# The first expert-choice call's norm, scores and choice of tokens for four sequences, worked out among units 47 to 68 of the mixture ahead of it

## The chip, the cores and the metric

The kernel is one program on one core of a Trainium2 chip. Its engines run side by side, each in the order of its own instruction list: TensorE (PE, matmuls and transposes into PSUM), VectorE (DVE), ScalarE (ACT), GpSimd (POOL) and SyncE (SP, which issues DMAs). They wait for one another only at semaphores. The metric is device time in microseconds (us), lower is better. Kernels are compared by the median of several runs. Where it ran, a profiled execution gives the time of each instruction.

## The reference

2048 tokens (8 sequences of 256) of width 128 go through six layers: a mixture of experts, a linear attention, the same mixture again, an expert-choice layer, a causal attention, and the expert-choice layer again. Every layer has a layer norm ahead of it and is added to the stream `x`. The second mixture and the first expert-choice call are the place of this change:

```python
x = x + 0.5 * _L0_ffn_ref(_layernorm(x, axis=-1), ...)   # 8 routed experts, 2 per token, and a shared one
x = x + 0.5 * _L1_ffn_ref(_layernorm(x, axis=-1), ...)   # expert choice
...
def _L1_ffn_ref(x, gate_w, w1, w2):
    scores = jnp.einsum('ntd,ed->nte', x, gate_w)
    probs = jax.nn.softmax(scores, axis=-1)
    g, m = jax.lax.top_k(probs.transpose(0, 2, 1), k)     # each expert takes 64 of a sequence's 256 tokens
    xin = x[batch_idx, m]
    h = jnp.einsum('nekd,edf->nekf', xin, w1)
    ...
```

A sequence's choice depends on that sequence's tokens alone, so four of the eight sequences can be chosen as soon as the mixture has finished those four.

## The kernel before

The stream lies as `xr`, 128 features by 2048 tokens, in four blocks of 512 tokens (two sequences each). An instruction such as "128x512" covers one block.

**The mixture** is `ffn0`, called twice. Its work is a list of 72 units: 8 of the shared expert, then 16 for each block in order (8 experts, two halves of the hidden width). A unit goes round all engines. PE does `up` (six matmuls, `L128` to `L130`), ScalarE a silu (`gate`, `L1290`), VectorE multiplies it with the second product (`product`, `L1755`) and by the token's weight (`weigh`, `L1762`), ScalarE rounds it to the matmul's short form (`high`, a cast, `L1299`), GpSimd subtracts to get the rest (`L2174`), and PE does `down` (three matmuls) four units later. `up(n)` waits until `product(n - 2)` has emptied its PSUM banks. When a block's last unit is down, VectorE adds the block to `xr` (`add`, `L1766`): block 0 behind the product and weighing of unit 29, block 1 of unit 45, block 2 of unit 61, block 3 after the end.

**The first expert-choice call** is `ffn1`, and its head already stands at the end of the second `ffn0`. For a block it needs: centred tokens (`ln_centre`, a matmul), their square and a copy (ScalarE, `ln_square`, `ln_copy`), the variance and the gate's scores (`ln_variance` and `scores` on PE, many narrow matmuls), and the tokens turned round and scaled (`rows_turned` on PE, then ScalarE, then a subtraction on GpSimd). For four sequences (a part, blocks 0 and 1 or 2 and 3) it then needs: the inverse root (`ln_root`, eleven small operations of VectorE) and the scores less their maximum (`part_weights`), the exponential (ScalarE, which has to load another table of functions), the division (`chances`), a transpose on PE, and the choice on VectorE: `top_start`, eight `top_rounds` of three operations each (the eight largest, their places, and their removal), `top_end`. PE turns the result back (`tops`) and spreads it (`indices`), VectorE copies it into columns (`columns`) and makes the one-hot matrices (`select`), and with these PE picks the tokens (`gather`), from which the experts' matmuls start.

Before, the head for blocks 0 and 1 starts at units 68 and 69 of the mixture (centre on PE, square and copy on ScalarE); variance and scores stand between the last four downs; everything from the root on comes after the last unit, and 28 `spare` matmuls, whose results nobody reads, stand ahead of `tops`.

The order on each engine is the order in which its function issues the instructions, so the position of a call in a loop is the only thing that sets it. The numbers after "L" in rows of before are lines of the kernel printed here.

## Time and profile before

| | |
|---|---|
| median of 3 runs | 1073.49 us (1071.27 to 1079.22) |
| profiled execution, its own time | 1074.08 us |
| its span on the core | 1072.4 us |
| PE busy | 959.2 us (89%) |
| VectorE busy | 706.4 us (66%) |
| ScalarE busy | 619.3 us (58%) |
| GpSimd busy | 338.7 us (32%) |

A busy share is a mean over stages with different limits. The second mixture lies between about 493 and 651 us, the join to the expert-choice call between about 640 and 684 us. A row of the timeline gives the start, the length, the engine, the line, the operation, its output and inputs and their sizes; what ended the engine's idle time stands in brackets. Matmul rows overlap, because matmuls are pipelined: their starts tell the pace. fp32 matmuls count twice in the trace where they take two passes, so 8 narrow ones are "x16". A row that covers several instructions runs from the start of the first to the end of the last.

### The profile page before, as it was taken

What the parts mean: (1) busy time and instruction counts of PE and PEld (TensorE: products, weight loads), DVE (VectorE), ACT (ScalarE), POOL (GpSimd) and SP (SyncE); (2) the same over time, 40 slices, a digit from 0 to 9 for tenths busy, and PEclk for the clock granted to TensorE, in tenths of its full rate; (3) what the DMA queues carried; (4) which work ended last, traced back from release to release, by engine and by line L of the source; (5) the groups of instructions that cost most, each with busy time, mean ns of one, the idle gap of its engine ahead of it and who ended that gap; (6) DMA issues with size and microseconds to landing.
All of it is one profiled execution on the core that took longest, in us unless ns stands there. A gap on an engine that the chain in (4) does not pass through costs nothing.

```text
span 1072.4 us, 13356 instructions
## 1 busy us (share of the span) xinstructions
PE 959.2 (89%) x4674; PEld 636.4 (59%) x4674; DVE 706.4 (66%) x1413; ACT 619.3 (58%) x1003; POOL 338.7 (32%) x249
## 2 busy tenths in 40 slices
PE   8899999889999999889999998899977878787997
PEld 5678887333333333357888875688544545454886
DVE  3978887577877787546888877634375455438532
ACT  6555555378888888653555553635644545445454
POOL 1697777100000000003777764201201211123200
PEclk9999999999999999888999998899988888889999
DMA  5225120000000000004321211100000000001001
GB/s 173 50 76 162 60 66 23 0 0 1 1 1 1 0 1 1 0 1 135 76 67 59 63 37 60 40 2 1 1 2 2 4 2 2 4 1 40 1 1 40
DMA packets 30745, 33.66 MB, mean 31 GB/s; under 512 B 2063, under 2 KB 19799, under 8 KB 30679
## 3 DMA queue, kind: packets, MB, share of 16 engines
q1 hardware_dynamic: 30678, 32.81, 10.6%
q8 instruction: 37, 0.61, 0.2%
q14 instruction: 30, 0.24, 0.1%
HBM read 31.36 MB, written 1.18 MB: 30 GB/s over the span
## 4 chain that ended last, share of the span: by engine, by line
PE 50%; DVE 20%; ACT 11%; POOL 11%; issue 8%; DMA 0%; SPq 0%; ACTq 0%; POOLq 0%; DVEq 0%
POOL fl L2174 9%; PE ps L128 6%; PE ps L129 6%; PE ps L130 6%; PE ps L760 5%; PE ps L878 4%; PE ps L754 2%; ACT ex L1504 2%; ACT L1393 2%; PE ps L738 2%; DVE smax L2053 2%; PE ps L972 2%; PE ps L907 1%; DVE stk L2045 1%; PE ps L981 1%
## 5 line engine op out<-in xcount | busy, mean ns | idle before, releaser
L2174 POOL TENSOR_TENSOR fl<-fp,fh 128x512 fp32r<-128x512 f32 x144 | 224.1, 1573 | 123.5 <-ACT fh L1299 123.4
L1290 ACT ACTIVATE fs<-ps 128x512 f32<-128x512 f32 x144 | 86.3, 599 | 112.7 <-PE ps L130 112.5
L1762 DVE TENSOR_TENSOR fp<-fp,cwb 128x512 f32<-128x512 f32 x128 | 140.3, 1096 | 14.0 <-DVE fp L1755 0.9
L1755 DVE TENSOR_TENSOR fp<-fs,ps 128x512 f32<-128x512 f32 x144 | 98.1, 682 | 39.4 <-ACT fs L1290 39.0
L128 PE MATMUL ps<-z_hi,w_hi 128*128 128x512 f32 x288 | 116.4, 404 | 3.3 <-DVE fp L1755 3.3
L129 PE MATMUL ps<-z_lo,w_hi 128*128 128x512 f32 x288 | 115.7, 402 | 0.0
L130 PE MATMUL ps<-z_hi,w_lo 128*128 128x512 f32 x288 | 115.2, 400 | 0.0
L1299 ACT CAST fh<-fp 128x512 fp32r<-128x512 f32 x144 | 88.8, 617 | 35.4 <-DVE fp L1762 31.0
L2238 POOL TENSOR_TENSOR ln_sq<-ln_rs 128x512 f32<-128x512 f32 x20 | 21.4, 1069 | 264.8 <-ACT ln_rs L1356 264.8
L2231 POOL TENSOR_SCALAR_AFFINE_SELECT ex<-ex 128x1024 f32<-128x1024 f32 (+1 forms) x24 | 33.4, 1403 | 158.5 <-ACT ex L1504 158.5
L2053 DVE TENSOR_REDUCE smax<-ps 128x8 f32<-128x2048 f32 (+1 forms) x24 | 54.9, 2290 | 42.0 <-PE ps L986 33.9
L878 PE MATMUL ps<-hid,w 128*128 128x256 f32 x256 | 67.3, 387 | 0.0
L128 PEld LDWEIGHTS ps<-z_hi,w_hi 128*128 128x128 f32 x288 | 55.2, 192 | 18.8 <-DVE fp L1755 5.5
L754 PE MATMUL ps<-z,wb 128*128 128x512 f32 x128 | 62.8, 618 | 2.7 <-DVE qq L1859 2.7
L1440 ACT ACTIVATE hid<-ps 128x512 f32<-128x512 f32 x64 | 38.0, 597 | 46.5 <-PE ps L130 45.7
L130 PEld LDWEIGHTS ps<-z_hi,w_lo 128*128 128x128 f32 x288 | 55.4, 192 | 12.9
L129 PEld LDWEIGHTS ps<-z_lo,w_hi 128*128 128x128 f32 x288 | 55.1, 191 | 12.5 <-issue 0.2
L128 PE MATMUL ps<-fh,w_hi 128*128 128x512 f32 x144 | 57.6, 400 | 2.9 <-POOL fl L2174 2.9
L760 PE MATMUL ps<-hid,wb 128*128 128x512 f32 x128 | 60.1, 593 | 0.0
L129 PE MATMUL ps<-fl,w_hi 128*128 128x512 f32 x144 | 56.9, 395 | 0.0
L130 PE MATMUL ps<-fh,w_lo 128*128 128x512 f32 x144 | 56.8, 394 | 0.0
L742 PE MATMUL ps<-ln_sq,mean_w 128*128 128x512 f32 x72 | 39.4, 629 | 18.7 <-ACT ln_sq L1349 18.7
(272 smaller groups left out, 2037.1 us busy)
## 6 DMA issues: line engine op xcount, KB each, us to landing
cwb<-cw_spread SPq DMA_DIRECT2D x64, 256.0 KB, 3.1
w_raw<-in_L_ffn_w_dram SPq DMA_DIRECT2D x20, 256.0 KB, 3.1
w_raw<-in_L_ffn_w_dram SPq DMA_DIRECT2D x4, 512.0 KB, 5.7
w<-in_L_ffn_w_dram SPq DMA_DIRECT2D x8, 256.0 KB, 4.8
x_tok<-in_L_attn_x_dram SPq DMA_DIRECT2D x4, 256.0 KB, 3.6
wb<-in_L_attn_W_dram SPq DMA_DIRECT2D x1, 1024.0 KB, 7.0
wb<-in_L_attn_W_dram SPq DMA_DIRECT2D x4, 256.0 KB, 3.9
out_dram<-z SPq DMA_DIRECT2D x4, 256.0 KB, 3.0
```

Of the source, the lines that this page charges most:

```text
L128: pe.matmul(out, w_hi, x_hi, start=start, stop=False)
L129: pe.matmul(out, w_hi, x_lo, start=False, stop=False)
L130: return pe.matmul(out, w_lo, x_hi, start=False, stop=stop)
L754: pe.matmul(ps[:, bank, :], wb[:, b, (4 + k) * P:(5 + k) * P], blk(z, t), start=True, stop=True).then_inc(a0_matmul[t], 1)
L760: pe.matmul(ps[:, A0_WO, :], wb[:, b, w], hid[:, k, :], start=(k == 0), stop=(k == FT - 1)).then_inc(a0_matmul[t], 1)
L878: ins = pe.matmul(ps[:, OUT1[n % 2], 0:SEQ], w2[:, e, ft * P:(ft + 1) * P], hid[:, g % RING1, f * SEQ:(f + 1) * SEQ], start=(ft == 0), sto ...
L1290: act.activation(fs[:, n % 2, :], ps[:, n % 2, :], ACT.Silu).then_inc(silu_done, 1)
L1299: act.copy(fh[:, n % RING0, :], fp[:, n % RING0, :]).then_inc(fhi_done, 1)
L1755: dve.tensor_tensor(f, fs[:, n % 2, :], ps[:, 2 + n % 2, :], ALU.mult).then_inc(prod_done, 1)
L1762: dve.tensor_tensor(f, f, cwb[:, x % CW_RING, :], ALU.mult).then_inc(weighed, 1)
L2053: dve.tensor_reduce(smax[:, s % 2, int(k > 0), :, hgs], ps[:, bank:bank + 4, :].rearrange("p g (h t) -> p g h t", h=HG if k == 0 else 2), ...
L2174: pool.tensor_tensor(fl[:, n % RING0, :], fp[:, n % RING0, :], f32(fh[:, n % RING0, :]), ALU.subtract).then_inc(flo_done, 1)
```

## The change

A constant `EARLY1 = 47` is added. The head for blocks 0 and 1 (part 0) of the first expert-choice call moves into the units from 47 on: centre on PE in unit 47, square and copy on ScalarE in 48 and 49, variance in 50, scores in 51, root and part weights on VectorE behind the weighing of 52, the exponential on ScalarE in 53 with a table load before and one behind it, chances in 54, their transposes in 55, the start of the choice in 56, its eight rounds in 57 to 64 (one behind each weighing), its end in 65, the transposes back in 67, and the columns in 68. After the last unit the transposed rows, `indices` and the head for blocks 2 and 3 are interleaved anew on PE and ScalarE, and the 28 spare matmuls are gone. The result of `tops` for part 0 lies in PSUM bank 5 instead of 3.

```diff
-        PT_AT, GI_AT = ((5, 3), (2, 3)), (3, 5)
+        PT_AT, GI_AT = ((5, 3), (2, 3)), ((5, 5), (3, 5))
...
+                elif call == 0 and n == 1:
+                    pe.wait_ge(col_done, part1(call, i) + 1)
...
-                    if call == 1 and n == ALL0 - 4:
+                    if call == 1 and n == EARLY1:
                         ln_centre(LN_FFN1, 0)
                         ln_centre(LN_FFN1, 1)
+                    if call == 1 and n == EARLY1 + 3:
+                        pe.wait_ge(lxc_copied, later(LN_FFN1, 1))
+                        ln_variance(LN_FFN1, 0)
+                        ln_variance(LN_FFN1, 1)
+                    if call == 1 and n == EARLY1 + 4:
+                        scores(LN_FFN1, 0)
+                        scores(LN_FFN1, 1)
+                    if call == 1 and n == EARLY1 + 8:
+                        chances(0, 0)
+                    if call == 1 and n == EARLY1 + 20:
+                        tops(0, 0)
...
                 if call == 1:
                     pe.wait_ge(prod_done, U + ALL0)
                     rows_turned(0, LN_FFN1, 0)
+                    indices(0, 0)
                     rows_turned(0, LN_FFN1, 1)
+                    indices(0, 1)
                     ln_centre(LN_FFN1, NTB - 1)
                     ln_variance(LN_FFN1, 2)
                     scores(LN_FFN1, 2)
-                    chances(0, 0)
                     ln_variance(LN_FFN1, NTB - 1)
                     scores(LN_FFN1, NTB - 1)
-                    spare(GI_AT[0], 28)
-                    tops(0, 0)
-                    indices(0, 0)
-                    indices(0, 1)
...
-                    if call == 1 and n == ALL0 - 3:
-                        for tb in range(SPB):
-                            ln_square(LN_FFN1, tb)
-                            ln_copy(LN_FFN1, tb)
+                    if call == 1 and n in (EARLY1 + 1, EARLY1 + 2):
+                        ln_square(LN_FFN1, n - EARLY1 - 1)
+                        ln_copy(LN_FFN1, n - EARLY1 - 1)
+                    if call == 1 and n == EARLY1 + 6:
+                        act.preload_act_table_set(LN_EXP)
+                        chances(0, 0)
+                        act.preload_act_table_set("silu_and_others")
...
                 if call == 1:
+                    rows_turned(0, LN_FFN1, 0)
                     ln_square(LN_FFN1, 2)
                     ln_copy(LN_FFN1, 2)
-                    act.preload_act_table_set(LN_EXP)
-                    chances(0, 0)
+                    rows_turned(0, LN_FFN1, 1)
                     ln_square(LN_FFN1, NTB - 1)
                     ln_copy(LN_FFN1, NTB - 1)
-                    rows_turned(0, LN_FFN1, 0)
-                    rows_turned(0, LN_FFN1, 1)
+                    act.preload_act_table_set(LN_EXP)
...
-                if call == 1:
-                    dve.wait_ge(sc_ready, part1(0, 0) + 1)
-                    ln_root(LN_FFN1, 0, SPB - 1)
-                    part_weights(0, LN_FFN1, 0)
+                    if call == 1 and n == EARLY1 + 5:
+                        dve.wait_ge(sc_ready, part1(0, 0) + 1)
+                        ln_root(LN_FFN1, 0, SPB - 1)
+                        part_weights(0, LN_FFN1, 0)
+                    if call == 1 and n == EARLY1 + 7:
+                        chances(0, 0)
+                    if call == 1 and n == EARLY1 + 9:
+                        top_start(0, 0)
+                    if call == 1 and n - EARLY1 - 10 in range(CAP // 8):
+                        top_rounds(0, 0, (n - EARLY1 - 10,))
+                    if call == 1 and n == EARLY1 + 18:
+                        top_end(0, 0)
+                    if call == 1 and n == EARLY1 + 21:
+                        columns(0, 0)
                 add(NTB - 1)
-                if call == 1:
-                    chances(0, 0)
-                    top_start(0, 0)
-                    top_rounds(0, 0, range(CAP // 8))
-                    top_end(0, 0)
...
-                columns(call, 0)
+                if call == 1:
+                    columns(call, 0)
                 select(0)
```

The first place is VectorE at the end of the mixture. Before, the last weighing is followed by root, part weights, the add of block 3 (`L1766`), chances and the choice; `gates`, `gidx` and `tk` are the choice's values, places and work table.

```order
L1762 TENSOR_TENSOR fp<-fp,cwb 128x512
...
L1644 TENSOR_TENSOR sce<-ps,ln_r 128x64
L1647 TENSOR_REDUCE scm<-sce 128x8
L1649 TENSOR_TENSOR sce<-sce,scm 128x64
L1766 SCALAR_TENSOR_TENSOR xr<-ps,xr 128x512
L1655 TENSOR_REDUCE scs<-sce 128x8
...
L1674 COPY tk<-ps 32x256
L1684 MAX gates<-tk 32x8
L1686 MAX_INDEX gidx<-gates,tk 32x8
L1688 MATCH_REPLACE tk<-gates,tk 32x256
```

Of the change, in the round units (57 and 58 are shown), one round stands behind each product and weighing:

```order
L1761 TENSOR_TENSOR fp<-fs,ps 128x512
L1768 TENSOR_TENSOR fp<-fp,cwb 128x512
L1690 MAX gates<-tk 32x8
L1692 MAX_INDEX gidx<-gates,tk 32x8
L1694 MATCH_REPLACE tk<-gates,tk 32x256
L1761 TENSOR_TENSOR fp<-fs,ps 128x512
L1768 TENSOR_TENSOR fp<-fp,cwb 128x512
L1690 MAX gates<-tk 32x8
```

The rounds, one block behind the last weighing before, are spread over eight units, and the next product of the mixture waits in VectorE's list behind each.

The second place is ScalarE. Before, the exponential of `sce` and its table load stand behind the last cast of the mixture, ahead of the turned rows (`xtf`, `xt_hi`):

```order
L1299 CAST fh<-fp 128x512 x2
L1245 ACTIVATE ln_sq<-ps 128x512
L1249 COPY z<-ps 128x512
L1334 ACT_TABLE_LOAD
L1258 ACTIVATE sce<-sce 128x64
L1245 ACTIVATE ln_sq<-ps 128x512
L1249 COPY z<-ps 128x512
L1267 ACTIVATE xtf<-ps,ln_r 128x128 x4
L1271 CAST xt_hi<-xtf 128x512
L1267 ACTIVATE xtf<-ps,ln_r 128x128 x4
```

Of the change, around unit 53 (the first silu, `fs`, is unit 53's, the one behind the loads is unit 54's):

```order
L1294 ACTIVATE fs<-ps 128x512
L1303 CAST fh<-fp 128x512
L1330 ACT_TABLE_LOAD
L1262 ACTIVATE sce<-sce 128x64
L1332 ACT_TABLE_LOAD
L1294 ACTIVATE fs<-ps 128x512
```

The exponential has moved in front of unit 54's silu, with a second load that was not there.

The third place is PE behind the mixture. Before (`L602` turns rows, `L571` centres, `L578` is the variance, `L594` the scores, `L566` a spare matmul, `L618` turns the choice back, `L634` spreads it, `L849` gathers):

```order
L602 MATMUL ps<-ident,z 128x128 x8
L571 MATMUL ps<-xr,centre 128x512
L578 MATMUL ps<-mean_w,ln_sq 128x1 x4
L594 MATMUL ps<-par,z 128x8 x4
L609 MATMUL ps<-ident,prb 32x128 x2
L578 MATMUL ps<-mean_w,ln_sq 128x1 x4
L594 MATMUL ps<-par,z 128x8 x4
L566 MATMUL ps<-ident_b 128x512 x28
L618 MATMUL ps<-ident,gates 128x32
L618 MATMUL ps<-ident,gidx_f 128x32
L634 MATMUL ps<-blockd,nsel 128x512 x2
L566 MATMUL ps<-ident_b 128x512 x5
```

Of the change:

```order
L603 MATMUL ps<-ident,z 128x128 x4
L637 MATMUL ps<-blockd,nsel 128x512
L603 MATMUL ps<-ident,z 128x128 x4
L637 MATMUL ps<-blockd,nsel 128x512
L572 MATMUL ps<-xr,centre 128x512
L579 MATMUL ps<-mean_w,ln_sq 128x1 x4
L595 MATMUL ps<-par,z 128x8 x4
L579 MATMUL ps<-mean_w,ln_sq 128x1 x4
L595 MATMUL ps<-par,z 128x8 x4
L567 MATMUL ps<-ident_b 128x512 x5
L853 MATMUL ps<-onehot,xt_hi 128x512 x2
```

What spreads the choice now stands between the turned rows; variance and scores of blocks 2 and 3 are what remains between them and the first gather.

## Rows read from the trace of the kernel before

**Rows 1.** Windows: length, busy PE, PEld, DVE, ACT, POOL, clock, DMA.
```profile
44.00:52.00 8.00, 6.30 (x27) 4.75 (x26) 7.72 (x9) 4.28 (x8) 6.71 (x4) 1.00 0.35 61
...
600.00:620.00 20.00, 20.00 (x88) 16.18 (x87) 16.54 (x21) 10.97 (x19) 15.05 (x10) 1.00 0.20 61
...
682.00:684.00 2.00, 0.00 (x0) 0.00 (x0) 1.90 (x8) 1.97 (x7) 1.57 (x2) 1.00 0.00 0
...
684.00:686.00 2.00, 1.93 (x8) 1.87 (x9) 1.93 (x8) 1.90 (x4) 2.00 (x2) 0.57 0.00 0
```

**Rows 2.** Groups by line, 516 to 634: shapes, count; busy, mean ns; idle before.
```profile
L2174 POOL TENSOR_TENSOR fl<-fp,fh 128x512 fp32r<-128x512 f32 x57 | 89.6, 1590 | 29.4 <-ACT fh L1299 29.4
...
L1762 DVE TENSOR_TENSOR fp<-fp,cwb 128x512 f32<-128x512 f32 x57 | 62.2, 1092 | 6.3 <-DVE fp L1755 0.5
...
L1299 ACT CAST fh<-fp 128x512 fp32r<-128x512 f32 x57 | 35.1, 616 | 12.0 <-DVE fp L1762 12.0
```

**Rows 3.** Timeline, VectorE, second mixture: start, length, line, operation.
```profile
593.30 0.69 DVE L1762 TENSOR_TENSOR fp<-fp,cwb 128x512 f32<-128x512 f32 x1
...
593.91 0.68 DVE L1755 TENSOR_TENSOR fp<-fs,ps 128x512 f32<-128x512 f32 x1
...
594.70 1.01 DVE L1762 TENSOR_TENSOR fp<-fp,cwb 128x512 f32<-128x512 f32 x1
...
602.87 0.67 DVE L1755 TENSOR_TENSOR fp<-fs,ps 128x512 f32<-128x512 f32 x1
...
644.64 0.68 DVE L1755 TENSOR_TENSOR fp<-fs,ps 128x512 f32<-128x512 f32 x1
```

**Rows 4.** Timeline, GpSimd and VectorE, early in the second mixture, small operations.
```profile
500.66 1.44 POOL L2174 TENSOR_TENSOR fl<-fp,fh 128x512 fp32r<-128x512 f32 x1 [0.23 <-ACT fh L1299]
...
500.66 1.59 DVE L1742 TENSOR_TENSOR oh<-iota_e,ixf 128x128 f32<-128x128 f32 x2
...
502.28 0.49 DVE L1746 TENSOR_TENSOR oh<-oh,pr 128x128 f32<-128x128 f32 x2
```

**Rows 5.** Timeline, PE, end of the second mixture and join.
```profile
635.43 1.88 PE L571 MATMUL ps<-xr,centre 128*128 128x512 f32 x4
...
644.12 1.84 PE L578 MATMUL ps<-mean_w,ln_sq 128*128 128x1 f32 x16
...
650.40 0.39 PE L130 MATMUL ps<-fh,w_lo 128*128 128x512 f32 x1
...
670.42 1.41 PE L849 MATMUL ps<-onehot,xt_hi 128*128 128x512 f32 x2
...
677.75 0.73 PE L849 MATMUL ps<-onehot,xt_hi 128*128 128x512 f32 x2 [0.84 <-DVE onehot L1928]
```

**Rows 6.** Timeline, VectorE, at the join behind the second mixture.
```profile
648.48 0.17 DVE L1612 TENSOR_SCALAR ln_v<-ps 128x8 f32<-128x8 f32 x1 [2.37 <-PE ps L594]
...
651.49 0.68 DVE L1766 SCALAR_TENSOR_TENSOR xr<-ps,xr 128x512 f32<-128x512 f32 x1
...
655.37 0.41 DVE L1674 COPY tk<-ps 32x256 f32<-32x256 f32 x1 [1.78 <-PE ps L609]
...
655.93 0.42 DVE L1684 MAX8 gates<-tk 32x8 f32<-32x256 f32 x1
...
666.73 0.68 DVE L1699 TENSOR_TENSOR blockd<-gidx_f,m 32x512 bf16<-32x512 f32 x1
...
668.30 0.17 DVE L1709 COPY icol<-ps 64x16 f32<-64x16 f32 x1
```

**Rows 7.** Timeline, GpSimd, at the join.
```profile
659.21 4.94 POOL L2191 TENSOR_TENSOR w_lo<-w_raw,w_hi 128x512 fp32r<-128x512 f32 x4
```

**Rows 8.** Timeline, ScalarE, at the join.
```profile
651.23 1.28 ACT L1334 ACT_TABLE_LOAD   x1
...
652.52 0.26 ACT L1258 ACTIVATE sce<-sce 128x64 f32<-128x64 f32 x1
...
654.34 1.16 ACT L1267 ACTIVATE xtf<-ps,ln_r 128x128 f32<-128x128 f32 x4
```

12 lines of the change are left out of this document (3 added, 9 removed).

## The prediction

> **What bounds the kernel now.** I read the groups of the second mixture first, then windows, then the timeline engine by engine over the join behind it. In the mixture's steady part PE is never idle (20.00 of 20 us) and VectorE is busy 16.54 of 20 [rows 1]: 57 units in 118 us, 2.07 us each, set by PE's nine matmuls [rows 2]. VectorE's busy share holds waiting as well as work: from weighing to product it is 0.61 us and from product to weighing 0.79, 1.40 for a unit [rows 3], but the weighing takes 1.09 us on the mean and 0.69 where nothing is in its way [rows 2, 3], so 0.40 us of each is waiting. What it waits for is GpSimd's subtraction (1.59 us each, three quarters of the unit): two small operations of VectorE that started with one of 1.44 us took 1.59, while two of the same size right behind it took 0.49 [rows 4].
>
> The join is the opposite: nothing is dense. The last down of the mixture ends at 650.40 + 0.39 = 650.79 and the first gather starts at 670.42 [rows 5], 19.6 us later. In between VectorE works alone: root and weights from 648.48 to 651.49, then the choice from 655.37 to 667.41 [rows 6]. This is what the change takes out of the join. The question is what it costs where it goes.
>
> **What is moved, and its price on VectorE.** Root and part weights 3.0 us; chances 0.8 (estimate: four small operations, 0.2 each from the 0.17 of the root's first); start of the choice 0.56; eight rounds with their two copies 10.80, `blockd` 0.68; columns, four copies of 0.17, 0.6; with the add of block 2, which was there before and is 0.68, 17.1 us stand beside the 20 units 52 to 71 [rows 6]. At 0.67 us of slack a unit (2.07 - 1.40) they could hide 13.4 at the very best; with the 0.40 of waiting, 5.4. So VectorE, not PE, sets the pace from unit 52 on. A round unit then takes about 1.40 + 1.35 = 2.75 us. The rounds themselves run beside GpSimd undisturbed: in the join they kept their pace under four subtractions of GpSimd [rows 6, 7].
>
> **PE's share.** The centring of blocks 0 and 1 (1.7 us) moves from unit 68 to 47 and is paid in both. Variance and scores, 16 small matmuls each and 1.7 us each [rows 5], leave the tail and go into units 50 and 51. By unit 52 the new kernel is 3 x 1.7 = 5.1 us behind; that is slack in which VectorE loses its backlog, for which I take 0.8 us (estimate: two mean waits of 0.40). Unit 52's product, at 602.87 before (its row names no wait for ScalarE, so VectorE was late there), so starts near 602.87 - 0.8 + 5.1 = 607.2 [rows 3].
>
> **From there to the product of unit 71.** 19 units at 1.40 are 26.6; the moved work 17.1; waiting behind GpSimd 0.40 in the 11 units without a round, 4.4 [rows 2] (in a round unit the subtraction falls under the round: weighing 0.69, cast 0.62 and a subtraction, 1.24 each where four ran alone and 1.59 here, make 2.6 to 2.9, about the unit); the root's and `blockd`'s two-input operations under a running subtraction, 1.8 (bounds 0 and 3, from the 1.1 us lost in [rows 4]). Then bubbles at units 53 to 56, 3.0: ScalarE does the exponential between two table loads, and the silu of unit 54 comes only after the second, 0.26 + 1.28 + 0.6 = 2.1 us behind the part weights, while VectorE has only product and weighing of 53 to do, 1.4: it waits 0.7. PE first waits in up(55) for the product of 53, which stands behind root and weights (4.2 us with a subtraction in the way, of which PE has two units' lead, so about 2.2), then at the transposes of unit 55 until VectorE has product, weighing and chances of 54 (2.2 and a wait of 1, less its own 0.7 of down: about 2.5). That holds back up(56), another 0.4, and probably costs a few us at the lower clock: after 682 to 684, where PE did nothing, the clock was 0.57 of full in the next 2 us [rows 1]. I put 1.9 there (bounds 0 and 9, below). Sum 52.9: the product of unit 71 starts near 660.1, before it was 644.64 [rows 3]: +15.5.
>
> The first load costs nothing, since the roots cover it; without that cover it would be 1.3 us more. In this trace a load is 1.28 us and the exponential starts 0.01 us behind it [rows 8]. The Trainium skill, page "ScalarE: Activation LUTs", section "What ACT_TABLE_LOAD costs", puts a drain of about 1.38 us behind each load, 2.66 in all. By that the second load would hold the silu 1.4 us longer, and the time would be 1079; the row shows no such gap, and I go by the row.
>
> **The waits that it adds, and who stands behind them.** PE's variance in unit 50 waits for ScalarE's copy of unit 49; ScalarE has two squares and two copies more in units 48 and 49, about 1.0 us a unit beside two instructions of 0.6, so it just keeps the pace. ScalarE's exponential waits for the part weights, and behind it stand the second load, the silu of 54 and the cast of 53, for which GpSimd and then PE wait. PE's transposes of unit 55 wait for the chances, with up(56) behind them. The transposes of the choice in unit 67 and the columns in 68 find their sources done two units earlier. SP's and GpSimd's own instructions keep their order, and the weights that they load and split at the join follow the mixture's end.
>
> **The tail.** Before, product 71 to the end of the last down took 650.79 - 644.64 = 6.15 us, with variance and scores in it. Without them the chain is product and weighing 0.79 + 0.69, cast 0.7, subtraction 1.59, three matmuls 0.9: 4.7. The mixture's end moves by 15.5 - 1.4 = +14.1.
>
> **The new join.** After the last down PE turns block 0 (0.5), and then ScalarE sets the time: turned rows of block 0 (1.16 and a cast, 1.8), square and copy of block 2 (two at about 0.5), turned rows of block 1 (1.8), square and copy of block 3 (1.0) [rows 2, 8]. PE's scores of block 3 wait for that copy and stand ahead of the gather in its order: 0.5 + 5.6 + 0.9, then five spare matmuls, about 1.8 with waits. The first gather so starts about 9.1 us after the last down instead of 19.6: -10.5. What is late next is therefore that copy, with scores, root and weights of block 3 behind it. From the first to the fourth gather it was 677.75 - 670.42 = 7.3 us [rows 5]. VectorE now waits there less for ScalarE (-1.5), but its second root falls under the four subtractions of `w_lo`, 4.94 us [rows 7], which the rounds had covered before without harm (+1.2). I take 0. The spare matmuls removed filled a wait and cost nothing.
>
> **Sum.** +14.1 - 10.5 = +3.6. The profiled execution took 1074.08 us, 0.6 above the median of 1073.49: 1077.7, so 1078.
>
> **The rivals.**
> - *The mixture swallows more (faster).* If no weighing falls under a subtraction from unit 52 on and there are no bubbles, the sum to product 71 is 26.6 + 17.1 = 43.7, the shift +6.3, at the end of the mixture +4.9, and with the 1.5 behind the gather 4.9 - 10.5 - 1.5 = -7.1: 1067. For it: slower units leave GpSimd time to finish in a round's shadow, and the weighing of 0.69 is common [rows 3]. Against it: the units between the moved pieces are as tight as before.
> - *PE's clock falls in the stretched units (slower).* With VectorE as the bound PE idles about a quarter of each round unit. If the clock goes to 1.2 GHz and stays there, a unit's nine matmuls take about 3.9 us instead of 2.1 (twice the spacing) and PE binds again at 3.9 against 2.75: 1.15 in each of eight units, +9.2, so 1087. It decides (over 1% slower) from about six such units. For it: the drop after the wait at 682 [rows 1]. Against it: from 44 to 52, in the first mixture, PE was also idle 1.70 of 8 us, and the clock stayed 1.00 [rows 1]. The Trainium skill, page "TensorE: Matmul & The Clock Gate", section "HAM oscillation — how this bites in real kernels", describes bursts of matmuls between waits that fall to the lower clock each time; this is that rule at work here, and the trace shows it only for the longer wait.
> - *The choice still ends last at the join (no change).* Then nothing is gained and the rest is as before, near 1074. VectorE works in order, so all of it is done before the weighing of unit 69; hardly possible.
>
> A bound beyond these: every one of 20 weighings waiting for two thirds of a subtraction, 1.06 us, would give 21 instead of 4.4, +17. The 57 units of [rows 2] wait 0.40 on the mean, so I leave that end outside the range.
>
> **How the numbers follow.** My forecast, the mixture paying what the join gains and a little more, 1072 to 1083: 0.55. The faster rival, 1063 to 1072: 0.22. The slower, 1083 to 1092: 0.20. No change by an idle move: 0.03. Runs of this kernel differ by up to 0.7%, so about 1% (10.7 us) is what can be told from no change. Under 1063 is reached only with a gain beyond the faster rival's own sum: 0.03. Over 1084 is most of the slower one: 0.16. Between: 0.81. The range 1068 to 1088 takes in both rivals' sums nearly and leaves out about 0.2.
>
> **What would show it.** Right: rounds standing behind weighings at units 57 to 64, unit spacing of about 2.7 there; PE waiting for products of VectorE, which it never did in this mixture's middle; two waits of over 2 us near unit 55; the last down 14 us later; the first gather 9 us behind it, behind the scores of block 3; a GpSimd subtraction beside the second root. Wrong: unit spacing still 2.1 in the rounds (the faster rival), matmul spacing doubled over several units (the slower one), or a first gather that comes 12 us or more behind the last down because scores or turned rows are later than I think.

## The result, and the profile after

The changed kernel takes 1083.64 us in the median of 20 executions (1071.75 to 1086.52), the kernel before beside it 1075.57 us (1066.23 to 1082.61). The ratio is 1.0057 with a 95% interval of 1.0031 to 1.0083: slower, by less than 1%. The forecast was 1078 in a range of 1068 to 1088. Two executions of over 2.3 ms, one of the kernel before and one of a variant, are left out of every mean, count and level below.

| | before | after |
|---|---|---|
| profiled execution, its own time | 1074.08 us | 1071.75 us |
| its span on the core | 1072.4 us | 1070.0 us |
| mean granted clock of PE over the span | 0.951 | 0.958 |

So the profiled execution of the changed kernel is the quickest of its 20, quicker than that of before, while the usual one is slower by 8 us. One profile cannot explain that. The executions of the changed kernel lie in two groups, 1072 to 1078 us and 1083 to 1087 us, and the mean granted clock goes with them: 0.949 to 0.958 in the first, 0.939 to 0.944 in the second.

Windows of the changed kernel (length, busy PE, PEld, VectorE, ScalarE, GpSimd with their instructions, clock, DMA share, GB/s), for [rows 1]:

```profile
600.00:620.00 20.00, 16.46 (x81) 13.14 (x79) 14.07 (x28) 9.87 (x17) 7.83 (x6) 0.91 0.13 40
620.00:660.00 40.00, 36.91 (x151) 27.20 (x151) 36.81 (x82) 19.37 (x33) 21.61 (x16) 1.00 0.11 34
670.00:675.00 5.00, 4.80 (x20) 3.98 (x21) 1.15 (x2) 4.08 (x7) 3.43 (x3) 0.50 0.01 4
```

VectorE is now the dense engine of the mixture's end (36.81 of 40 us), PE waits a little in each unit (36.91 of 40) and keeps its 2.4 GHz there (1.00). The join runs at 1.2 GHz for a while (0.50).

VectorE of the changed kernel, timeline, for [rows 3, 6]: product of unit 52, one operation of the root, product of 53, three products of round units with a round's first operation between them, product of unit 71:

```profile
608.56 0.69 DVE L1761 TENSOR_TENSOR fp<-fs,ps 128x512 f32<-128x512 f32 x1 [1.53 <-ACT fs L1294]
...
611.87 1.15 DVE L1624 TENSOR_TENSOR ln_t<-ln_r 128x8 f32<-128x8 f32 x1
...
614.86 0.68 DVE L1761 TENSOR_TENSOR fp<-fs,ps 128x512 f32<-128x512 f32 x1
...
628.88 0.66 DVE L1761 TENSOR_TENSOR fp<-fs,ps 128x512 f32<-128x512 f32 x1
629.65 0.69 DVE L1768 TENSOR_TENSOR fp<-fp,cwb 128x512 f32<-128x512 f32 x1
630.25 0.41 DVE L1690 MAX8 gates<-tk 32x8 f32<-32x256 f32 x1
...
631.50 0.67 DVE L1761 TENSOR_TENSOR fp<-fs,ps 128x512 f32<-128x512 f32 x1
...
634.12 0.67 DVE L1761 TENSOR_TENSOR fp<-fs,ps 128x512 f32<-128x512 f32 x1
...
659.44 0.69 DVE L1761 TENSOR_TENSOR fp<-fs,ps 128x512 f32<-128x512 f32 x1
```

A round unit takes 2.62 us (631.50 - 628.88, 634.12 - 631.50), with the round's MAX8 right behind the weighing. PE of the changed kernel, for [rows 5]: its two waits near unit 55, the last down of the mixture, variance and scores of block 2 and then of block 3, spare matmuls, first and fourth gather:

```profile
615.59 0.80 PE L129 MATMUL ps<-z_hi,w_hi 128*128 128x512 f32 x1 [2.83 <-DVE fp L1761]
...
620.30 0.39 PE L610 MATMUL ps<-ident,prb 128*32 128x128 f32 x2 [1.01 <-DVE prb L1666]
...
664.33 0.39 PE L131 MATMUL ps<-fh,w_lo 128*128 128x512 f32 x1
...
667.53 1.05 PE L579 MATMUL ps<-mean_w,ln_sq 128*128 128x1 f32 x8
668.45 1.04 PE L595 MATMUL ps<-par,z 128*128 128x8 f32 x8
670.20 1.87 PE L579 MATMUL ps<-mean_w,ln_sq 128*128 128x1 f32 x8 [0.71 <-ACT ln_sq L1249]
671.93 1.86 PE L595 MATMUL ps<-par,z 128*128 128x8 f32 x8
673.63 2.29 PE L567 MATMUL ps<-ident_b 128*128 128x512 bf16 x5
...
675.37 1.38 PE L853 MATMUL ps<-onehot,xt_hi 128*128 128x512 f32 x2
...
683.34 1.19 PE L853 MATMUL ps<-onehot,xt_hi 128*128 128x512 f32 x2 [0.83 <-DVE onehot L1939]
```

The last down ends at 664.33 + 0.39 = 664.72, and the first gather follows 10.65 us behind it (before 19.63, [rows 5]). Block 3's variance and scores take 1.87 and 1.86 us where block 2's took 1.05 and 1.04, since the clock fell to 0.50 at about 670. Before it fell, PE had done block 2's narrow matmuls (128x1 and 128x8) and then waited 0.71 us. In the kernel before it fell at the same kind of place without a wait: PE was busy all the time, with the narrow matmuls of blocks 2 and 3 from 653 on and spare matmuls from 656.8:

```profile
653.00:656.00 3.00, 3.00 (x28) 2.80 (x27) 1.01 (x6) 2.58 (x7) 0.00 (x0) 1.00 0.00 0
...
657.00:660.00 3.00, 3.00 (x8) 1.03 (x7) 2.83 (x12) 2.89 (x6) 2.57 (x3) 0.50 0.01 3
```

Now VectorE's second root and GpSimd's subtractions beside it, for [rows 6, 7]:

```profile
673.82 0.17 DVE L1618 TENSOR_SCALAR ln_v<-ps 128x8 f32<-128x8 f32 x1 [5.58 <-PE ps L595]
674.02 1.12 DVE L1621 TENSOR_SCALAR ln_r<-ln_v 128x8 int32<-128x8 int32 x1
675.18 1.20 DVE L1624 TENSOR_TENSOR ln_t<-ln_r 128x8 f32<-128x8 f32 x1
676.41 1.20 DVE L1626 SCALAR_TENSOR_TENSOR ln_t<-ln_t,ln_v 128x8 f32<-128x8 f32 x1
677.65 0.17 DVE L1628 SCALAR_TENSOR_TENSOR ln_r<-ln_t,ln_r 128x8 f32<-128x8 f32 x1
```

```profile
672.63 4.97 POOL L2203 TENSOR_TENSOR w_lo<-w_raw,w_hi 128x512 fp32r<-128x512 f32 x4 [1.57 <-ACT w_hi L1279]
```

Three operations of 0.17 us take 1.12, 1.20 and 1.20 while the four subtractions run; as these end at 672.63 + 4.97 = 677.60, the next takes 0.17 again. That is 3.0 us.

**Where the time goes, by landmarks.** An execution can run a few tenths to some us late already ahead of the change's place, so I measure from one silu to the next landmark. These are ScalarE's rows of the silu of unit 47, the attention's first vT, and the first gelu of the second expert call, first of before, then of the changed kernel's first profile:

```profile
591.01 0.60 ACT L1290 ACTIVATE fs<-ps 128x512 f32<-128x512 f32 x1 [0.33 <-PE ps L130]
...
790.45 0.69 ACT L1513 ACTIVATE vT<-ps,par 128x512 f32<-128x512 f32 x1 [5.81 <-PE ps L130]
...
991.07 0.59 ACT L1440 ACTIVATE hid<-ps 128x512 f32<-128x512 f32 x1
```

```profile
592.05 0.60 ACT L1294 ACTIVATE fs<-ps 128x512 f32<-128x512 f32 x1 [0.34 <-PE ps L131]
...
796.27 0.69 ACT L1519 ACTIVATE vT<-ps,par 128x512 f32<-128x512 f32 x1 [6.75 <-PE ps L131]
...
990.31 0.59 ACT L1446 ACTIVATE hid<-ps 128x512 f32<-128x512 f32 x1
```

The change's own stretch takes 199.44 us before and 204.22 after, +4.8. The attention behind it, in which no instruction differs, takes 200.62 before and 194.04 after, -6.6. (The changed kernel's profile is also 1.0 us later at unit 47 and 1.6 us shorter behind the last landmark, 79.7 instead of 81.3; together that is the 2.4 us between the two spans.) The first is the change; the second needed experiments.

### The profile page after: what moved, and what is told of

It is laid out like the page before. It is cut to its first block, busy times and chain, and to the rows that moved or that the text cites. A ratio compares the mean times of both kernels' runs of the same rounds, so it can differ in the third digit from the quotient of the medians.

```text
span 1070.0 us, 13293 instructions
## 1 busy us (share of the span) xinstructions
PE 949.2 (89%) x4638; PEld 629.8 (59%) x4646; DVE 707.2 (66%) x1413; ACT 622.1 (58%) x1005; POOL 333.8 (31%) x249
## 3 DMA queue, kind: packets, MB, share of 16 engines
q1 hardware_dynamic: 30678, 32.81, 10.5%
## 4 chain that ended last, share of the span: by engine, by line
PE 46%; DVE 19%; POOL 12%; ACT 12%; issue 10%; DMA 0%; SPq 0%; POOLq 0%; ACTq 0%; DVEq 0%
POOL fl L2186 10%; PE ps L129 5%; PE ps L130 5%; PE ps L764 5%; PE ps L131 5%; PE ps L882 4%; PE ps L758 2%; ACT ex L1510 2%; ACT L1399 2%; PE ps L742 2%; DVE smax L2065 2%; PE ps L976 1%; PE ps L911 1%; DVE stk L2057 1%; DVE ek L1865 1%
## 5 line engine op out<-in xcount | busy, mean ns | idle before, releaser
L2186 POOL TENSOR_TENSOR fl<-fp,fh 128x512 fp32r<-128x512 f32 x144 | 219.2, 1537 | 140.9 <-ACT fh L1303 140.7
```

The lines of the kernel that those rows point to most:

```text
L2186: pool.tensor_tensor(fl[:, n % RING0, :], fp[:, n % RING0, :], f32(fh[:, n % RING0, :]), ALU.subtract).then_inc(flo_done, 1)
```

## The experiments

The stretches of every kernel, from such rows of its own profile (us). "52" is the silu of unit 52 and so on, "add" the last add of the mixture, "gather" and "gelu" the first of the expert call, "vT" the attention's first, "gelu 2" the first gelu of the second expert call. From the first gelu to vT the code is the same in every kernel but delay2 and delay5, and it takes 105.5 to 108.1 us; a difference of 1 or 2 us in "47 to vT" can come from there:

| kernel | 47 to 52 | 52 to 56 | 56 to 65 | 65 to 71 | 71 to add | add to gather | gather to gelu | gelu to vT | 47 to vT | vT to gelu 2 |
|---|---|---|---|---|---|---|---|---|---|---|
| before | 10.44 | 8.37 | 18.84 | 14.27 | 8.56 | 18.93 | 12.92 | 107.11 | 199.44 | 200.62 |
| before_again | 10.46 | 8.38 | 18.83 | 14.28 | 8.56 | 18.93 | 12.92 | 106.99 | 199.35 | 197.02 |
| changed | 15.88 | 14.19 | 22.88 | 13.81 | 5.95 | 10.61 | 14.42 | 106.48 | 204.22 | 194.04 |
| again | 15.88 | 15.55 | 22.86 | 13.80 | 5.98 | 10.51 | 14.53 | 106.52 | 205.63 | 204.33 |
| pool_late | 15.88 | 14.17 | 22.88 | 13.80 | 5.95 | 10.61 | 11.43 | 106.42 | 201.14 | 202.88 |
| half_rate | 15.89 | 14.18 | 20.23 | 12.72 | 8.42 | 10.54 | 14.37 | 108.05 | 204.40 | 200.65 |
| choice_late | 15.88 | 14.19 | 18.84 | 12.56 | 6.88 | 19.53 | 14.14 | 106.53 | 208.55 | 204.26 |
| choice_free | 15.88 | 15.56 | 19.09 | 12.56 | 6.20 | 11.46 | 12.47 | 105.71 | 198.93 | 200.88 |
| join_tight | 15.88 | 15.56 | 22.86 | 13.81 | 5.96 | 7.15 | 13.20 | 105.45 | 199.87 | 203.40 |
| tight | 15.87 | 15.56 | 20.24 | 12.71 | 6.80 | 8.37 | 12.47 | 107.24 | 199.26 | 204.09 |
| spaced | 15.88 | 13.69 | 20.74 | 13.97 | 6.64 | 8.22 | 12.28 | 107.30 | 198.72 | 200.97 |
| no_load | 15.89 | 13.12 | 22.94 | 13.80 | 5.95 | 9.91 | 14.77 | 108.12 | 204.50 | 193.85 |
| delay2 | 15.89 | 14.17 | 22.87 | 13.80 | 5.95 | 10.61 | 14.29 | 108.53 | 206.11 | 195.50 |
| delay5 | 15.89 | 14.18 | 22.88 | 13.80 | 5.94 | 10.62 | 14.45 | 110.70 | 208.46 | 193.44 |

And the times of those that were timed, with the ratio to the executions of before that stand beside each. "Low clock" counts the executions with a mean granted clock of 0.945 or less. "At 0.95" is read off straight lines, time against mean clock, one level for each kernel and one common slope: 7.5 us for each 0.01 of clock, with a scatter of 1.0 us.

| kernel | median us | lowest to highest | ratio, 95% interval | low clock | at 0.95 |
|---|---|---|---|---|---|
| before (beside the experiments) | 1076.2 | 1064.2 to 1082.4 | | 32 of 87 | 1074.7 |
| changed and again | 1083.6, 1084.1 | 1071.8 to 1086.5 | 1.0057, then 1.0105 [1.0059, 1.0152] | 19 of 26 | 1078.0, 1078.1 |
| choice_late | 1087.3 | 1077.1 to 1088.4 | 1.0112 [1.0042, 1.0182] | 3 of 4 | 1079.4 |
| half_rate | 1074.8 | 1071.8 to 1082.9 | 1.0012 [0.9969, 1.0055] | 2 of 9 | 1076.7 |
| pool_late | 1078.2 | 1070.1 to 1081.2 | 1.0020 [0.9976, 1.0064] | 1 of 10 | 1077.7 |
| join_tight | 1073.5 | 1066.6 to 1081.2 | 0.9994 [0.9945, 1.0044] | 3 of 10 | 1074.2 |
| tight | 1077.3 | 1072.0 to 1079.9 | 1.0010 [0.9971, 1.0048] | 6 of 10 | 1071.2 |
| choice_free | 1074.4 | 1068.8 to 1079.7 | 1.0010 [0.9965, 1.0055] | 3 of 10 | 1073.7 |
| delay2 | 1083.2 | 1074.2 to 1086.4 | 1.0072 [1.0029, 1.0115] | 5 of 10 | 1080.2 |
| spaced | 1073.8 | 1065.5 to 1079.0 | 0.9990 [0.9952, 1.0027] | 4 of 12 | 1073.0 |
| delay5 | 1077.3 | 1075.6 to 1083.5 | 1.0034 [1.0003, 1.0065] | 0 of 12 | 1080.9 |

The level at 0.95 is a rough measure: pool_late, whose stretch is 3.1 us shorter than the changed kernel's, lies 0.3 under it, and tight, whose stretch is that of before, 3.5 under before. So I judge the variants by their stretches.

**again: the changed kernel once more, for a profile of the usual execution.**

> The changed kernel once more, nothing edited; its times lie in two groups, 1072 to 1078 and 1083 to 1087, and its first profile is of the quicker group. Theory A (the mixture and the join do the same in every execution; the groups come from the attention behind them): in a profile of about 1084 the product of unit 71 starts within 1 us of 659.4, the first gelu of the experts (hid) near 690, the first vT of the attention near 796, and what is more lies between 800 and 990, at a lower granted clock than the 0.83 to 0.91 of the first profile. Theory B (the clock of PE falls in the stretched units of the mixture or at the join in the usual execution): the clock is under 0.8 over several us between 620 and 690, the product of unit 71 starts at 664 or later or the first gelu at 695 or later.

Its profiled execution took 1084.61 us. Mixture and join are those of the first profile but for 1.4 us at units 52 to 56, and the first vT is at 797.19: theory A. What makes this execution longer lies behind. The window 790 to 990 of the first profile, of again, and of the first profile of before:

```profile
790.00:990.00 200.00, 153.68 (x1491) 100.63 (x1499) 116.94 (x202) 95.38 (x115) 42.03 (x31) 0.87 0.03 8
```

```profile
790.00:990.00 200.00, 158.29 (x1460) 100.91 (x1461) 109.95 (x173) 87.49 (x96) 40.97 (x30) 0.81 0.03 8
```

```profile
790.00:990.00 200.00, 156.56 (x1466) 100.62 (x1464) 112.97 (x196) 94.80 (x113) 41.26 (x31) 0.85 0.03 8
```

The columns are those above. At a clock of 0.81 instead of 0.87 VectorE got through 173 instructions of the attention instead of 202 in the same 200 us. The 1.4 us at units 52 to 56 are clock too. PE in again, the transposes of unit 55 and behind them the first two matmuls of up(56):

```profile
619.78 0.61 PE L610 MATMUL ps<-ident,prb 128*32 128x128 f32 x2 [1.73 <-DVE prb L1666]
620.04 0.78 PE L129 MATMUL ps<-z_hi,w_hi 128*128 128x512 f32 x1
620.62 0.63 PE L130 MATMUL ps<-z_lo,w_hi 128*128 128x512 f32 x1
```

There the matmuls run at 0.63 us instead of 0.39 from 616.6, 1.5 us behind the end of a wait of 2.82, until about 623.5, with the wait of 1.73 in between. That is the slower rival's mechanism, but in two units and not in eight, and 1.4 us dearer than in the first profile, not 9.

**before_again: the kernel before once more.**

> The kernel before once more, nothing edited. From the silu of unit 47 to the first vT of the attention: 199.4 us in its first profile, 204.2 and 205.6 in two of the changed kernel; from there to the first gelu of the second expert call 200.6, and 194.0 to 204.3 over nine profiles of its variants. Theory A (the first stretch is the kernel's own, the second is left to the clock): first stretch within 1 us of 199.4, the second anywhere from 194 to 205, and the mean clock follows it. Theory B (both belong to the kernel): second stretch within 1 us of 200.6.

The first stretch is 199.35 us (199.44 in the first profile), the attention 197.02 instead of 200.62, and the execution took 1070.05 us at a mean clock of 0.956. So the change's stretch is repeatable to 0.1 us in the kernel before, and the attention is not the kernel's own: theory A.

**pool_late: GpSimd's subtractions away from the second root.**

```
                 if call == 0:
+                    pool.wait_ge(prb_ready, part1(0, 1) + 1)
                     for e in range(EXP // 2):
                         split_low(e)
```

> GpSimd's first four subtractions of w_lo wait until VectorE has the chances of the second part; else the changed kernel. Theory A (the second root and weights, 5.4 us instead of 2.1, are held up by the four subtractions, and are the chain to the first gelu): the three operations of 1.12 to 1.20 us take 0.17, root and weights end about 3 us earlier, the first gelu near 687 instead of 690, the kernel 2.5 to 3 us quicker than the changed one. Theory B (gathers and ScalarE's copies bind there): first gelu within 1 us of 690, no difference; a loss of up to 2 us if the first up of the experts now waits for w_lo.

VectorE at the same place:

```profile
675.20 0.17 DVE L1621 TENSOR_SCALAR ln_r<-ln_v 128x8 int32<-128x8 int32 x1
675.41 0.17 DVE L1624 TENSOR_TENSOR ln_t<-ln_r 128x8 f32<-128x8 f32 x1
675.61 0.17 DVE L1626 SCALAR_TENSOR_TENSOR ln_t<-ln_t,ln_v 128x8 f32<-128x8 f32 x1
```

All three take 0.17 us. From the first gather to the first gelu it is 11.43 us instead of 14.42, and all of it reaches the attention: 201.14 instead of 204.22 from the silu of 47 to the first vT, -3.1. Theory A, in size too. The medians differ by more (1078.2 against 1084.1), and the levels at 0.95 by less (0.3); the 3.0 us are read from the stretch and its rows.

**half_rate: a round in every second unit.**

```
-                    if call == 1 and n - EARLY1 - 10 in range(CAP // 8):
-                        top_rounds(0, 0, (n - EARLY1 - 10,))
-                    if call == 1 and n == EARLY1 + 18:
-                        top_end(0, 0)
-                    if call == 1 and n == EARLY1 + 21:
-                        columns(0, 0)
+                    if call == 1 and n - EARLY1 - 10 in range(0, CAP // 4, 2):
+                        top_rounds(0, 0, ((n - EARLY1 - 10) // 2,))
+                if call == 1:
+                    top_end(0, 0)
                 add(NTB - 1)
+                if call == 1:
+                    columns(0, 0)
```

(PE's transposes of the choice then stand behind the last down.)

> A round in every second unit (57, 59 to 71) instead of one in each of 57 to 64; the choice's end and its columns behind unit 71. Theory A (a unit has about 0.67 us of slack on VectorE, two of them hide a round of 1.35): product of unit 71 at 651 to 656 instead of 659.4, last down and first gather 3 to 8 us earlier, the kernel 3 to 8 us quicker than the changed one. Theory B (a round costs its own time wherever it stands): product of unit 71 at 658 to 661, then the choice's end behind it, no gain or 2 us slower.

Theory A holds for the units: 56 to 71 take 32.95 us instead of 36.69, as much as in the kernel before (33.11). (The 33.11 hold the centring of blocks 0 and 1, which now stands in unit 47. choice_late below, with no round in the units, takes 31.40, so the seven rounds here cost 1.6 us in all.) So two units' slack does hide most of a round. But the tail gives 2.5 of the 3.7 us back (71 to add 8.42 instead of 5.95): the last round and the choice's end stand between product and add, and PE waits there and falls to the lower clock:

```profile
662.16 0.57 PE L129 MATMUL ps<-fh,w_hi 128*128 128x512 f32 x1 [2.10 <-POOL fl L2185]
662.52 0.63 PE L130 MATMUL ps<-fl,w_hi 128*128 128x512 f32 x1
```

The whole stretch, 204.40, is that of the changed kernel; the 1.4 us that are left of the gain at the first gelu go between there and the attention (108.05 instead of 106.48), where no instruction differs. Its median of 1074.8 us goes with only 2 of 9 executions at the low clock.

**choice_late and choice_free: only the early part among the units.** In choice_late the eight rounds, their end and the columns stand behind unit 71, and 28 spare matmuls again ahead of the transposes of the choice:

```
+                if call == 1:
+                    top_rounds(0, 0, range(3))
                 add(NTB - 1)
+                if call == 1:
+                    top_rounds(0, 0, range(3, CAP // 8))
+                    top_end(0, 0)
+                    columns(0, 0)
...
                     scores(LN_FFN1, NTB - 1)
+                    spare(3, 28)
+                    tops(0, 0)
+                    indices(0, 0)
+                    indices(0, 1)
```

> The early part stays among the units (norm, scores, root, weights, chances); the eight rounds, their end and the columns go back behind unit 71, with the 28 spare matmuls ahead of the transposes of the choice. Theory A (a round in a unit costs the mixture nearly its own time, VectorE being the bound): without 12.6 us of choice the units are bound by PE again, product of unit 71 at 648 to 650 instead of 659.4, the choice ends near 663, first gather 666 to 668 instead of 675.4, whole kernel about 8 us quicker than the changed one. Theory B (the rounds lie in VectorE's idle time, and the shift of 13.8 us comes from the waits at units 52 to 56): product of unit 71 at 655 or later, the choice behind it about 12 us, the whole kernel 5 us slower than the changed one or more.

The product of unit 71 starts at 653.60, between the two theories: with the rounds gone, units 56 to 65 take 18.84 us, exactly as before, and what stays lost is 47 to 56 (30.07 us instead of 18.81). So of the mixture's cost the rounds are 4.0 us (56 to 65), the choice's end and the columns 1.2 (65 to 71), and the early part is 11.3. The join went wrong in a way that neither theory had. VectorE's end of the choice, and PE's spares:

```profile
668.27 1.65 DVE L1705 TENSOR_TENSOR blockd<-gidx_f,m 32x512 bf16<-32x512 f32 x1
```

```profile
667.89 9.05 PE L567 MATMUL ps<-ident_b 128*128 128x512 bf16 x28
```

The choice ended at 668.27 + 1.65 = 669.92, and the spares, which filled a wait in the kernel before, stood in front of its transposes until 676.9. choice_free is choice_late without them and with the line of pool_late:

> choice_late without its 28 spare matmuls, and with GpSimd's four subtractions behind the chances of the second part. In choice_late the spares stood until 676.87 while the choice had ended at 669.9. Theory A (the spares held up the transposes of the choice): first gather 7 to 9 us earlier than in choice_late (679.4), silu of unit 47 to the first gelu 91 to 94 instead of 102.0. Theory B (the choice itself ends last): less than 4 us earlier, stretch 98 or more.

The first gather is at 672.34 instead of 679.38, 7.0 us earlier, the silu of 47 to the first gelu 93.22: theory A. Up to the first gelu that is 0.9 more than before (92.33), up to the first vT, 198.93, it is 0.5 less. So with the choice where it was, and GpSimd's subtractions out of the root's way, moving the early part alone gains about what it costs, within the 1 or 2 us that this measure can tell.

**join_tight and tight.** join_tight has pool_late's line, no spares ahead of the first gather, and block 3's norm ahead of turning block 1:

```
                     ln_copy(LN_FFN1, 2)
-                    rows_turned(0, LN_FFN1, 1)
                     ln_square(LN_FFN1, NTB - 1)
                     ln_copy(LN_FFN1, NTB - 1)
+                    rows_turned(0, LN_FFN1, 1)
...
                     indices(0, 0)
+                    ln_centre(LN_FFN1, NTB - 1)
                     rows_turned(0, LN_FFN1, 1)
                     indices(0, 1)
-                    ln_centre(LN_FFN1, NTB - 1)
```

> The mixture as in the changed kernel; at the join GpSimd's first four subtractions wait for the chances of the second part (as in pool_late), the five spare matmuls ahead of the first gather are gone, ScalarE squares and copies block 3 ahead of the turned rows of block 1, and PE centres block 3 ahead of turning block 1. Measured from the silu of unit 47 to the first gelu: before 92.3 us, changed kernel 97.7 and 99.1 in two profiles, pool_late 94.7. Theory A (scores of block 3, then the second root, are the chain): scores of block 3 end 2 us earlier, the spares' 1.7 us fall away, stretch 91 to 92.5, kernel 2 to 3.5 us quicker than pool_late. Theory B (ScalarE's copies of the gathered rows bind): stretch 94 to 95, no gain over pool_late.

The gather came 3.5 us earlier than in pool_late (add to gather 7.15 instead of 10.61), and 1.8 us of it went again on the way to the gelu (13.20 instead of 11.43). The total, 94.42 us to the first gelu, is theory B's number, but by the wrong road: units 52 to 56 happened to take 1.4 us more here, and from the silu of 56 on the gain is 1.7 us (62.98 against 64.67), less than the 2.2 to 3.7 of A. tight adds half_rate's order and 8 spares in the tail's wait:

> All of join_tight, with the rounds in every second unit as in half_rate, and 8 spare matmuls on PE in its wait of the tail (after the third last down). Silu of unit 47 to the first gelu: half_rate 96.4, pool_late 94.7. Theory A (the gains of the mixture and of the join add up): 88.5 to 90.5, below the 92.3 of before, so the kernel 2 to 4 us quicker than before where the attention takes the same. Theory B (what the mixture gains is lost in its tail, where the choice's end stands between the last weighing and the join): 92 to 95, no quicker than join_tight.

92.02 us to the first gelu: within theory B's 92 to 95, but 2.4 less than join_tight, where B saw no gain. The units gain 3.7 us against join_tight, the tail loses 0.8 and the way to the gather 1.2, and the way from there to the gelu is 0.7 shorter.

**no_load: no table loads in unit 53.**

```
-                        act.preload_act_table_set(LN_EXP)
-                        chances(0, 0)
-                        act.preload_act_table_set("silu_and_others")
+                        chances(0, 0, ACT.Silu)
```

> The changed kernel without the two table loads in unit 53: the exponential of the first part's chances is left out, ScalarE's silu stands in its place (the tokens chosen are others, the work is the same). From the silu of unit 52 to that of 56: before 8.4 us, changed kernel 14.2 and 15.6. Theory A (root and weights on VectorE ahead of the product of 53 make most of it, the loads only the 0.8 us that the product of 54 waited): 12.8 to 14.8 us, and PE's wait of 2.8 us for the product of 53 is still there. Theory B (the loads, 2.6 us, hold up the silu of 54 and all behind it): 12 us or less.

Units 52 to 56 take 13.12 us instead of 14.19, and PE's wait is still there:

```profile
618.07 0.79 PE L129 MATMUL ps<-z_hi,w_hi 128*128 128x512 f32 x1 [2.82 <-DVE fp L1759]
```

Theory A: the loads are 1.1 us of the 5.8 that these units lost. The other 4.7 hold VectorE's root and weights ahead of one product and the lower clock behind PE's wait (the next matmuls take 0.63 us instead of 0.39); no run takes these apart.

**spaced: tight with the early part spread over more units.**

```
                         ln_root(LN_FFN1, 0, SPB - 1)
+                    if call == 1 and n == EARLY1 + 6:
                         part_weights(0, LN_FFN1, 0)
-                    if call == 1 and n == EARLY1 + 7:
+                    if call == 1 and n == EARLY1 + 9:
                         chances(0, 0)
```

(ScalarE's exponential moves from unit 53 to 55, PE's transposes from 55 to 58, the rounds to 59, 61, 62, 64, 65, 67, 68 and 70.)

> tight with the early part spread over more units: root behind unit 52, weights behind 53, exponential and loads in 55, chances behind 56 and their transposes in 58, rounds at 59, 61, 62, 64, 65, 67, 68 and 70. Theory A (PE's waits of 2.8 and 1.7 us come from so much VectorE work standing ahead of one product): silu of 52 to silu of 56 9.5 to 11.5 us instead of 15.6, silu of 47 to the first vT 195 to 197.5 instead of 199.3 (before 199.4), the kernel 2 to 4 us quicker than before on the mean. Theory B (the same VectorE time is paid wherever it stands): what the first units gain the later ones lose, 198.5 to 200.5.

Theory B: 198.72 us. Units 52 to 56 came out at 13.69, and the two loads, no longer under the root, now held up a silu and with it VectorE:

```profile
621.37 0.69 DVE L1765 TENSOR_TENSOR fp<-fs,ps 128x512 f32<-128x512 f32 x1 [2.77 <-ACT fs L1298]
```

With 1073.8 us and a ratio of 0.9990 [0.9952, 1.0027] spaced cannot be told from the kernel before, and neither can any of the five other variants whose interval holds 1. No variant is shown to be quicker than before.

**delay2 and delay5: a later start of the attention, by table loads alone.** Two and four more table loads on ScalarE in the norm ahead of it:

```
                     act.preload_act_table_set(LN_EXP)
+                    for _ in range(extra):
+                        act.preload_act_table_set(LN)
+                        act.preload_act_table_set(LN_EXP)
```

> The changed kernel with two more table loads on ScalarE in the norm ahead of the attention (1.28 us each), nothing else: a delay of 2.6 us ahead of the attention and no other work. Of 26 executions of the changed kernel 19 had a mean clock of 0.945 or less, of the kernel before 9 of 22. Theory A (how much of the attention falls to the lower clock depends on when it starts, not on what the change does to it): the share of executions at the lower clock changes, to half or less, and the median moves by another amount than the delay, to 1074 to 1081. Theory B (the delay just adds): the share stays near three quarters and the median is 1085 to 1088.

> delay2 with twice the loads: four table loads more (5.1 us) on ScalarE in the norm ahead of the attention, nothing else changed. Executions with a mean clock of 0.945 or less: changed kernel 19 of 26, delay2 5 of 10 (median 1083.2 us, where the changed kernel has 1083.6 to 1084.1). Theory A (how many executions run the attention at the lower clock depends on when it starts): another share again, a quarter or less or nearly all, and a median off the line 1084 + 4.5, below 1085 or above 1090. Theory B (the delay just adds, and the share belongs to the change): three quarters of them at 0.945 or less, median 1087 to 1090.

The loads delay the first vT by 1.9 and 4.2 us (206.11 and 208.46 instead of 204.22). delay2 left it open: 5 of 10 executions at the low clock, and a median 0.5 to 0.9 below the changed kernel's. delay5 comes out as theory A says: none of 12 at the low clock (the lowest is 0.947), where the changed kernel has 19 of 26. Its median of 1077.3 is 6.4 to 6.8 us quicker than that of the kernel without the delay, its mean of 1078.7 3.5 us quicker. (The changed kernel was not run beside delay5. The kernel before was, and had 6 of 17 at the low clock there, 32 of 87 in all.) The windows 790 to 990 of delay5 and of choice_late, to be read beside the three above:

```profile
790.00:990.00 200.00, 152.31 (x1492) 99.93 (x1499) 118.32 (x197) 96.11 (x111) 41.02 (x30) 0.89 0.03 8
```

```profile
790.00:990.00 200.00, 157.17 (x1449) 100.27 (x1448) 109.80 (x171) 90.03 (x99) 40.88 (x30) 0.80 0.03 8
```

So a delay ahead of the attention, by table loads alone, changes how much of it runs at 1.2 GHz. That the start itself decides is not shown. Counted from the start of the program, choice_late starts the attention at 800.05 and takes 204.26 us for it, delay5 at 800.21 and takes 193.44. The loads also change PE's waits ahead of the attention: the two longest in the 40 us before it are 1.5 and 3.3 us in the changed kernel, 6.7 and 2.2 in delay5. These waits alone do not decide either, since the changed kernel's two profiles have the same ones and take 194.04 and 204.33.

## Why the prediction was right, and where its steps were off

The time lies in the range, and the first ratio, 1.0057, is within the 1% that was forecast (again's, 1.0105, is just outside). The sum and the median are two things, though. The median rose by 8.1 us (1075.57 to 1083.64), where the sum said 3.6, and it lies 0.6 us above the stretch of 1072 to 1083 that had most of the chance, in the slower rival's. That the range held it is in part luck.

The sum, +3.6 us, was for the change's own stretch. Against before, the two profiles of the changed kernel give (first profile, again):

| step | forecast | measured |
|---|---|---|
| end of the mixture | +14.1 | +12.9, +14.3 |
| last down to first gather, instead of 19.6 | 9.1 (-10.5) | 10.65, 10.55 (-9.0, -9.1) |
| first gather to first gelu | 0 | +1.5, +1.6 |
| first gelu to the attention | 0 | -0.6, -0.6 |
| sum | +3.6 | +4.8, +6.2 |

(The end of the mixture is 664.72 - 650.79, less the 1.04 us by which the silu of unit 47 was late already.) At equal mean clock the executions differ by 3.4 us, 1078.0 against 1074.7. That is less than 4.8, perhaps because the lower clock at units 55 to 56 and at the join counts as clock there.

Taken by its steps:

- **Round units of 2.75 us**: 2.62, at a clock of 1.00 as forecast, and PE waits in them for products of VectorE. The weighing there takes 0.69 us, as forecast.
- **Product of unit 52** at 607.2: 608.56, or 607.5 without the 1.04. **Product of unit 71** at 660.1: 659.44, or 658.4. Forecast +15.5, measured +13.8. Between the two products it is 50.9 us where the forecast's terms add up to 52.9. From silu to silu the rounds cost 4.0 us (choice_late) and the early part 11.3 (units 47 to 56). Of these 11.3, 5.4 come before unit 52, where the forecast had PE's 5.1 for the moved matmuls, and 5.8 in units 52 to 56.
- **Two waits of PE near unit 55 of 2.2 and 2.5 us**: 2.83 and 1.01 (1.73 in again). The lower clock behind them is there in both profiles. In the first, up to 618.3, it cost nothing: the transposes of unit 55 start 28.25 us behind the silu of unit 47 in it, and 28.22 in again, where up(55) ran at 2.4 GHz. In again it cost 1.4 us behind the transposes. The forecast had 1.9.
- **The table loads**: they cost 1.1 us (no_load), the forecast had 0.7 for the silu of 54. On the drain the trace of the changed kernel agrees with [rows 8]:

```profile
614.97 0.26 ACT L1262 ACTIVATE sce<-sce 128x64 f32<-128x64 f32 x1 [2.07 <-DVE sce L1655]
615.25 1.28 ACT L1332 ACT_TABLE_LOAD   x1
616.54 0.60 ACT L1294 ACTIVATE fs<-ps 128x512 f32<-128x512 f32 x1
```

  The load starts 0.02 us behind the exponential, and the silu 0.01 us behind the load. The Trainium skill, page "ScalarE: Activation LUTs", section "What ACT_TABLE_LOAD costs", adds a drain of about 1.38 us to each load; the measurement decides, and shows no gap on either side.
- **The tail** of 4.7 us: 5.28 (664.72 - 659.44). Too short by 0.6.
- **The first gather at 9.1 us**: 10.65. (The terms written there add up to 8.8: 0.5, 5.6, 0.9 and 1.8.) The copy of block 3 came as forecast, but its variance, its scores and the spares ran at 1.2 GHz (clock 0.50): 1.87 and 1.86 us against 1.05 and 1.04 for block 2. That is about 1.6 us, nearly the whole miss. The forecast had written the lower clock into unit 55 and not into the join, where the rows of before show it too: the first gather took 1.41 us, the fourth 0.73 [rows 5].
- **The second root under GpSimd, +1.2 at most**: this is the term that was mis-sized. It cost 3.0 us (pool_late takes back 3.1), and 1.5 of it stayed on the path to the first gelu after what ScalarE gained there. The bound had counted two-input operations under one subtraction, from [rows 4]. The trace shows three operations in a row, each ending within 0.03 us of the end of a subtraction (675.12, 676.35 and 677.59 one by one), the one with a single input (TENSOR_SCALAR, 1.12 us) as well. The Trainium skill, page "SBUF — State Buffer", section "Who interferes with whom", says that VectorE and GpSimd take a pair of ports from each other for a whole instruction, and names tensor_scalar among those that can, under conditions on its operands: the trace agrees.

The rivals: the faster one needed a mixture that ends 4.9 us later, and it ends 12.9 to 14.3 later. The third, a choice that still ends last at the join, did not come: its columns end ahead of the product of unit 69. The slower one's time, 1087, is near what came out, but its mechanism is not: in the rounds the clock stayed at 1.00, and the 1.2 GHz behind the waits at unit 55 lasted two units at most. The waits of 0.25 to 0.86 us in the round units did not bring the clock down, as this one of 0.26 and the 0.39 of the matmul behind the first show:

```profile
632.22 0.50 PE L129 MATMUL ps<-z_hi,w_hi 128*128 128x512 f32 x1 [0.26 <-DVE fp L1761]
632.56 0.39 PE L130 MATMUL ps<-z_lo,w_hi 128*128 128x512 f32 x1
```

The Trainium skill, page "TensorE: Matmul & The Clock Gate", section "HAM oscillation — how this bites in real kernels", describes bursts of matmuls that start at the lower clock behind each wait. The waits there are for DMAs and several times as long as those of the round units. The nearest to them here is the 2.83 us at unit 55, and behind it the trace agrees (0.63 us instead of 0.39).

What no step had is the attention. In the fourteen profiles here, what lies ahead of unit 47 takes 590.7 to 594.9 us and what lies behind the second expert call's first gelu 81.2 to 81.4 (79.7 in the changed kernel's first). The attention takes 193.4 to 204.3, and the share of executions at the low clock runs from 0 of 12 to about three quarters. The 26 executions of the changed kernel have a mean of 1082.2 us, 7.3 above the 1074.9 of before. By the two profiles 4.8 to 6.2 of that are the change's own stretch. The other 1.1 to 2.5, and the two groups of times, go with the clock behind it. What decides how much of the attention falls to 1.2 GHz stays open: a delay changed it (delay5), but no run here tells beforehand which kernel or which execution will be the quicker one.

## What to carry to other kernels

Moving work out of a serial join into a dense loop is paid in the loop, on the engine that becomes the bound: here 11.3 us for the early part (5.4 of them PE's) and 4.0 for the rounds, 12.9 at the loop's end, against about 9.0 won at the join. Cost what the moved work then runs beside in its new place, and what now follows it in the old one: a root that had run undisturbed came under GpSimd's subtractions for 3.0 us, and one wait on GpSimd took that back. Where a later stage runs at a clock that differs from execution to execution, judge a change by the stretch that it touches, from landmark to landmark: here the median moved by 8.1 us, the stretch by 4.8 to 6.2.
